# Adaptive-layernorm transformer block, float32, one core: the order of transposes and value matmuls in attention

## The chip, the cores and the metric
One Trainium2 chip, one of its cores. The time is that of the whole program on the device, in microseconds. Three runs of the kernel before gave 970.09, 970.40 and 970.41 us.

## What is computed
x has shape (2, 1024, 256). Cut to what matters:
```python
h = layernorm(x) * (1 + ca) + sa                    # modulation rows from silu(c) @ wmod
q, k, v = split(h @ wqkv.T)                         # 4 groups, 4 query heads each, D = 128
s = where(causal, q @ k.T / sqrt(128), -inf)        # per head 1024 x 1024
x = x + ga * (softmax(s) @ v) @ wproj.T
h = layernorm(x) * (1 + cb) + sb
x = x + gb * ffn(h)                                 # Hadamard transforms, silu gate, 256 -> 1024 -> 256
```
The attention takes from about 45 to 812 us of the span, the feed-forward part the rest.

## The kernel before
Every product is made of float32r pieces: an operand is split into a rounded high part and a low part, and the helper `three` (lines 930 to 935) adds high x high, high x low and low x high. So each tile that leaves TensorE is evicted twice: ACT copies the high part from PSUM, then DVE subtracts it from the same PSUM tile and writes the low part.

**Turns.** Attention runs in 8 turns t, one for each batch and key group. A turn has 8 row blocks i of 128 queries. Row block i has i+1 key blocks j. A unit n is one (row block, key block) pair with its four heads side by side, 512 columns; a turn has 36 units (`UNITS`). They are ordered by four windows of nine units, and window p holds the row blocks 7-p (big) and p (small): row blocks 7 and 0, 6 and 1, 5 and 2, 4 and 3.

**One list for all engines.** `walk` writes one list, `WALK`. TensorE, ACT, DVE and POOL each go through it in order and do their own part of every item, so the order of an engine's instructions follows from the list. The items:
- S (row block, head): TensorE multiplies queries with all keys of the row block (line 1039 and after). DVE adds the mask and takes the maximum (line 831, with a read of its accumulator). ACT does the exp and sums it (line 600). POOL takes the reciprocal and normalises. ACT does not do an exp at its item: `exps()` holds it back until the next S, or until just behind the next T.
- T (unit): TensorE waits until its PSUM bank is free and transposes four 128x128 tiles of probabilities (line 1054). ACT copies pt_hi (line 623), DVE subtracts pt_lo (line 835). There are two banks, used in turn, so a transpose needs the pt_lo of the unit two before it (`ring_free`). pt_hi and pt_lo have three buffers in SBUF.
- V (unit): TensorE waits for pt_lo and multiplies with the value block (lines 933 to 935). Behind the last unit of a row block ACT and DVE split the output (o_hi line 628, o_lo line 840).
- Y (row block): output projection, twelve matmuls of 256 columns, some values after the last V of that row block; DVE adds it to x (line 845).
- C (chunk): one projection of the next turn, six matmuls of 512 columns; VT: transposes of the values (line 1008).
- LF, LN, L, LH, LL: a piece of the second layernorm for two row tiles: statistics and normalisation on DVE, four transposes on TensorE at L (line 957, they use the same two PSUM banks as T), and their evictions.
- W, WM, WP, B: weight splits on POOL.

**The order around the change.** Window p gives each of its units up to two or three items to fill in between: in windows 0 to 2 the scores of the next window, in window 3 the chunks and first scores of the next turn. For a unit the list gets: the first fill item, T, the other fill items, and the V of the unit two before (`LAG` is 2). A V that ends a row block has its Y two values later. In the last turn window 3 has no chunks and no scores to fill in. The score of (i, head) waits in most cases for the exp two scores before, since two PSUM tiles hold scores.

Of the kernel before, what the change touches and what calls it, by code (L numbers as in the profile page):

```python
# [12 lines left out]
B, SEQ, HID = 2, 1024, 256  # L13
# [3 lines left out]
NT = SEQ // P  # L17
# [14 lines left out]
UNITS = []  # L32
for big, small in WINDOWS:
    UNITS += [(big, j) for j in range(HEAD)] + [(small, j) for j in range(small + 1)] + [(big, j) for j in range(HEAD, big + 1)]
NU = len(UNITS)
# [13 lines left out]
LAG = 2  # L49
# [12 lines left out]
CHUNKS_AT = (3, 3, 3, 3)  # L62


def walk():

    def scores(t, i):
        return [(t, "S", i, h) for h in range(QPG)]

    s7 = scores(0, NT - 1)
    out = [(0, "C", 0, 0), (0, "C", 1, 0), (0, "L0", 0, 0), (0, "C", 2, 0), (0, "LH0", 0, 0), (0, "C", 3, 0), (0, "M", 0, 0)]
    out += [(0, "C", c, 0) for c in (4, 5, 6)] + [(0, "G", 0, 0), (0, "C", 7, 0), (0, "WM", 0, 0), (0, "WP", 0, 0)]
    for h in range(QPG):  # L80
        out += [(0, "C", 8 + h, 0), s7[h]]
    for t in range(TURNS):
        s0, s6 = scores(t, 0), scores(t, NT - 2)
        rest = [(t - 1, "Y", i, 0) for i in WINDOWS[-1][::-1]] if t else []
        out += rest[:1] + [(t, "VT", 0, 0)] + s0[3 if t else 0:] + [s6[0]] + rest[1:]
        out += [(t, "WP", 0, 0)] if t else []
        behind, due = [], []

        def value():
            n = behind.pop(0)  # L90
            out.append((t, "V", n, 0))
            if due and due[0][0] == 1:
                out.append((t, "Y", due.pop(0)[1], 0))
            for row in due:
                row[0] -= 1
            if n == LAST[UNITS[n][0]]:
                due.append([3 if n >= NU - 3 else 2, UNITS[n][0]])

        for p, pair in enumerate(WINDOWS):
            units = [n for n, u in enumerate(UNITS) if u[0] in pair]  # L100
            fill = [[] for _ in units]
            if p + 1 < NW:
                for k, item in enumerate([item for i in WINDOWS[p + 1] for item in scores(t, i)][p == 0:]):
                    fill[k + (p == 0 and k > 1)].append(item)
            elif t + 1 < TURNS:
                left = [(t + 1, "C", c, 0) for c in range(NC)]
                for k, many in enumerate(CHUNKS_AT):
                    fill[k] += left[:many]
                    del left[:many]
                for h, item in enumerate(scores(t + 1, NT - 1) + scores(t + 1, 0)[:1]):  # L110
                    fill[len(CHUNKS_AT) + h].append(item)
                fill[1].append((t + 1, "WM", 0, 0))
            if p == 1:
                for k, what in ((0, "LF"), (3, "LN"), (5, "L"), (6, "LH"), (7, "LL")):
                    fill[k].append((t, what, 0, 0))
            if p == 2 and t + 1 < TURNS:
                fill[3].append((t, "W", 0, 0))
            if t + 1 == TURNS and p > 1:
                fill[2].append((t, "B", p - 2, 0))
            for n, extra in zip(units, fill):  # L120
                out += extra[:1] + [(t, "T", n, 0)] + extra[1:]
                behind.append(n)
                if len(behind) > LAG:
                    value()
        while behind:
            if len(behind) == LAG and t + 1 < TURNS:
                value()
                out += scores(t + 1, 0)[1:3]
            value()
        assert [i for _, i in due] == list(WINDOWS[-1][::-1])  # L130
    return out + [(TURNS - 1, "Y", i, 0) for i in WINDOWS[-1][::-1]]


WALK = walk()


# [20 lines left out]
def build(nc, x_in, wqkv, wproj, wmod, c_cols, wug, wdn, su_ug, su_dp, ws_ug, ws_dp, ident_in, mask_in, had_in, out):  # L157
    ctx = ExitStack()
    with ctx:
# [3 lines left out]
        def sem(name):  # L163
            return ctx.enter_context(nc.semaphore(name))
# [80 lines left out]
        T = [psum[2][:, 0:CH], psum[2][:, CH:2 * CH]]  # L245
# [29 lines left out]
        pv_done, oh_done, ol_done = sem("pv_done"), sem("o_hi_done"), sem("o_lo_done")  # L275
# [19 lines left out]
        def this(s, t, k):  # L295

            return (t + 1) * per[s.name] + k
# [11 lines left out]
        def ring(t, what, n=0):  # L309

            return T[TURNED.index((t, what, n)) % 2]
# [31 lines left out]
        def out_slot(i):  # L343

            return FINISHED.index(i) % 2
# [18 lines left out]
        W = [X if n == 1 else T for n in range(len(PIECES))]  # L364
# [56 lines left out]
        def _(pool):  # L421
# [13 lines left out]
            def ln_low(r, b, g, slot):  # L435

                n, block, _, _ = ln_step(r, b, g, slot)
                pool.wait_ge(ln[r]["hi"], n + LN_SLOTS[r] + 1)
                at = bass.ds(block * P, LP * P)
                g_.tensor_tensor(h_lo[:, :, at], h32[slot][:, :, :], h_hi[:, :, at].bitcast(F32), ALU.subtract).then_inc(ln[r]["lo"], 1)  # L440
# [103 lines left out]
        def _(act):  # L544
# [15 lines left out]
            def ln_modulate(r, b, g, slot):  # L560

                n, block, batch, which = ln_step(r, b, g, slot)
                shift, gain = SA + 3 * which, CA + 3 * which
                act.wait_ge(ln[r]["lo"], n + 1)
                act.wait_ge(ln[r]["tr"], n + LN_SLOTS[r] + 1)
                for k in range(KH):
                    last = a_.activation(h32[slot][:, k, :], ln_bank(r, b, g, slot)[:, k * LP * P:(k + 1) * LP * P], ACT.Identity,
                                         scale=cols[:, bass.ds(gain, 1), k, bass.ds(batch, 1)].rearrange("p a b -> p (a b)"),
                                         bias=cols[:, bass.ds(shift, 1), k, bass.ds(batch, 1)].rearrange("p a b -> p (a b)"))
                last.then_inc(ln[r]["h32"], 1)  # L570
# [4 lines left out]
            def v_high(t):  # L575
                for n in range(2):
                    act.wait_ge(vtr_done, this(vtr_done, t, n + 1))
                    a_.activation(v_hi[:, 4 * n:4 * n + 4, :].rearrange("p j d -> p (j d)"), ring(t, "VT", n), ACT.Copy).then_inc(v_hi_s, 1)

            def chunk(t, c):  # L580
                what, h, half = chunks(t)[c]
                act.wait_ge(qkv_done, this(qkv_done, t, c + 1))
                span = slice(half * CH, (half + 1) * CH)
                if what == "v":
                    a_.activation(vt[:, span], bank(t, c), ACT.Copy).then_inc(vt_done, 1)
                elif what == "k":
                    a_.activation(k_hi[:, span], bank(t, c), ACT.Copy).then_inc(qkv_hi, 1)
                else:
                    a_.activation(q_hi[:, h, span], bank(t, c), ACT.Copy, scale=SCALE).then_inc(qkv_hi, 1)  # L589
# [3 lines left out]
            def exps():  # L593

                while waiting:
                    t, i, h = waiting.pop(0)
                    nb, w = halves(i)

                    act.wait_ge(max_done, this(max_done, t, scored(i, h)))
                    a_.activation(row(i, h).rearrange("p (a n) -> p a n", a=nb),  # L600
                                  score_banks(i, h).rearrange("p (a n) -> p a n", a=nb)[:, :, 0:w],
                                  ACT.Exp, bias=nmax[:, place(i), h:h + 1], scale=-1.0,
                                  accum_out=rsum[:, place(i), h:h + 1]).then_inc(exp_done, 1)

            for t, what, n, h in WALK:
                if what == "C":
                    chunk(t, n)
                    exps()
                if what == "L0":
                    for slot in range(2):  # L610
                        ln_modulate(0, 0, 1, slot)
                if what == "VT":
                    exps()
                    v_high(t)
                if what == "L":
                    exps()
                    ln_modulate(1, t // NKV, t % NKV, 0)
                if what == "S":
                    exps()
                    waiting.append((t, n, h))  # L620
                if what == "T":
                    act.wait_ge(t_done, this(t_done, t, n + 1))
                    a_.activation(pt_hi[:, n % 3, :], ring(t, "T", n), ACT.Copy).then_inc(pth_done, 1)  # L623
                    exps()
                if what == "V" and n == LAST[UNITS[n][0]]:
                    i = UNITS[n][0]
                    act.wait_ge(pv_done, this(pv_done, t, n + 1))
                    a_.activation(o_hi[:, out_slot(i), :], O[i], ACT.Copy).then_inc(oh_done, 1)
# [579 lines left out]
```

## Time and profile before
| | us |
|---|---|
| median of three runs | 970.4 |
| the profiled execution, its own time | 970.33 |
| its span, first to last instruction | 968.5 |
| TensorE busy | 941.0 |
| DVE busy | 644.5 |
| ACT busy | 513.8 |
| POOL busy | 456.3 |

Busy time counts each instruction from its recorded start to its recorded end. Matmuls overlap in the records and their ends are modelled, so where a matmul's true length matters, the distance between starts is read. A line of the timeline gives start, length, engine, line of the kernel, operation, out<-in, shape, and how many instructions in a row it stands for; a bracket holds the idle time before it and what ended that.

### The profile page before, as it was taken

To read this page: it belongs to the slowest core of one execution; us is meant where nothing else is said; L and a number is where in the kernel's file an instruction comes from. 1 tells how busy PE (TensorE), PEld (TensorE's weight loads), DVE (VectorE), ACT (ScalarE), POOL (GpSimd) and SP (SyncE) were. 2 spreads that over 40 slices of the span, in tenths; PEclk is the share of its full clock that TensorE was granted. 3 is DMA by queue.
4 is the path that set the end of the run, shared out by engine and by line. 5 is a ranking of instruction groups with operands and counts; after the bars stand their busy time and mean duration, and the time that the engine had idled before them with its cause. 6 is when DMAs were issued, how large, how long until landed. Compare 5 with 4: busy or idle time off the path is not lost.

```text
span 968.5 us, 14525 instructions
## 1 busy us (share of the span) xinstructions
PE 941.0 (97%) x5344; PEld 817.9 (84%) x5344; DVE 644.5 (67%) x1302; ACT 513.8 (53%) x1069; POOL 456.3 (47%) x597
## 2 busy tenths in 40 slices
PE   5889999999999999999999999999999999999997
PEld 5779888988898889888988898889888987888885
DVE  6667757774777477757775777578747876864453
ACT  3266547654765476547654766476646665331121
POOL 1365707670767076707670767076707674120000
PEclk9899999999999999999999999999999999999999
DMA  8000000000001000100000001000000011000000
GB/s 307 23 1 1 33 1 23 2 33 1 23 1 34 1 23 1 33 1 23 1 34 1 23 1 33 1 23 2 1 1 1 1 48 51 1 20 3 22 22 22
DMA packets 9522, 21.14 MB, mean 22 GB/s; under 512 B 1264, under 2 KB 5488, under 8 KB 9328
## 3 DMA queue, kind: packets, MB, share of 16 engines
q1 hardware_dynamic: 8736, 20.19, 6.2%
q8 instruction: 40, 0.66, 0.3%
q14 instruction: 26, 0.21, 0.1%
q10 hardware_dynamic: 720, 0.08, 0.1%
HBM read 18.17 MB, written 2.10 MB: 21 GB/s over the span
## 4 chain that ended last, share of the span: by engine, by line
PE 89%; DVE 7%; ACT 3%; issue 1%; DMA 0%; POOL 0%; DVEq 0%; SPq 0%; ACTq 0%
PE ps L933 19%; PE ps L935 18%; PE ps L934 18%; PE ps L1054 11%; PE ps L1039 7%; PE ps L1045 6%; PE ps L1042 6%; DVE ps L831 3%; ACT prob L600 2%; DVE pt_lo L835 1%; PE ps L957 1%; PE ps L1008 1%; PE ps L1099 1%; PE ps L1100 0%; DMA x<-in_x 0%
## 5 line engine op out<-in xcount | busy, mean ns | idle before, releaser
L493 POOL TENSOR_TENSOR rinv<-rsum,mone 128x1 f32<-128x1 f32 x256 | 142.8, 558 | 274.7 <-ACT prob L600 274.7
L623 ACT ACTIVATE pt_hi<-ps 128x512 fp32r<-128x512 f32 x288 | 171.7, 596 | 134.5 <-PE ps L1054 133.6
L835 DVE TENSOR_TENSOR pt_lo<-ps,pt_hi 128x512 fp32r<-128x512 f32 x288 | 198.2, 688 | 64.3 <-ACT pt_hi L623 62.7
L600 ACT ACTIVATE prob<-ps,nmax 128x1024 f32<-128x1024 f32 (+7 forms) x256 | 189.6, 741 | 81.5 <-DVE nmax L831 80.7
L831 DVE CUSTOM_DVE_ANT_0 ps<-ps,mask_f 128x1024 f32<-128x1024 f32 (+7 forms) x256 | 193.8, 762 | 52.4 <-PE ps L1045 50.6
L496 POOL TENSOR_SCALAR prob<-prob,rinv 128x1024 f32<-128x1024 f32 (+7 forms) x256 | 191.4, 748 | 53.3 <-POOL rinv L493 53.3
L1054 PE MATMUL ps<-ident,prob 128*128 128x128 f32 x1152 | 171.1, 272 | 0.0
L1054 PEld LDWEIGHTS ps<-ident,prob 128*128 128x128 f32 x1152 | 141.1, 140 | 19.1
L933 PE MATMUL ps<-pt_hi,v_hi 128*128 128x512 f32 x288 | 134.3, 466 | 0.0
L935 PE MATMUL ps<-pt_hi,v_lo 128*128 128x512 f32 x320 | 126.3, 395 | 0.0
L1039 PE MATMUL ps<-k_hi,q_hi 128*128 128x512 f32 (+4 forms) x384 | 114.2, 352 | 9.6 <-ACT prob L600 6.7
L934 PE MATMUL ps<-pt_lo,v_hi 128*128 128x512 f32 x288 | 113.5, 394 | 0.0
L1045 PE MATMUL ps<-k_hi,q_lo 128*128 128x512 f32 (+4 forms) x384 | 111.5, 344 | 0.0
L1042 PE MATMUL ps<-k_lo,q_hi 128*128 128x512 f32 (+4 forms) x384 | 110.9, 343 | 0.0
L1039 PEld LDWEIGHTS ps<-k_hi,q_hi 128*128 128x128 f32 x384 | 70.2, 190 | 26.0 <-ACT prob L600 10.8
L794 DVE SCALAR_TENSOR_TENSOR q_lo<-ps,q_hi 128x512 fp32r<-128x512 f32 x64 | 44.1, 691 | 61.0 <-ACT q_hi L589 61.0
L933 PE MATMUL ps<-h_hi,w_hi 128*128 128x512 f32 x192 | 79.3, 413 | 2.8 <-DVE h_lo L747 2.8
L589 ACT ACTIVATE q_hi<-ps 128x512 fp32r<-128x512 f32 x64 | 38.3, 598 | 75.9 <-PE ps L935 75.9
L1042 PEld LDWEIGHTS ps<-k_lo,q_hi 128*128 128x128 f32 x384 | 71.3, 190 | 7.8
L935 PE MATMUL ps<-h_hi,w_lo 128*128 128x512 f32 x192 | 76.3, 397 | 0.0
L934 PE MATMUL ps<-h_lo,w_hi 128*128 128x512 f32 x192 | 76.2, 397 | 0.0
L1045 PEld LDWEIGHTS ps<-k_hi,q_lo 128*128 128x128 f32 x384 | 70.8, 189 | 5.3
(134 smaller groups left out, 1612.8 us busy)
## 6 DMA issues: line engine op xcount, KB each, us to landing
w_raw<-in_wqkv SPq DMA_DIRECT2D x8, 768.0 KB, 4.2
wp_raw<-in_wproj SPq DMA_DIRECT2D x8, 512.0 KB, 3.5
x<-in_x SPq DMA_DIRECT2D x4, 512.0 KB, 10.3
prob<-in_wug SPq DMA_DIRECT2D x4, 512.0 KB, 4.9
out_y<-prob SPq DMA_DIRECT2D x4, 512.0 KB, 2.9
prob<-in_wmod SPq DMA_DIRECT2D x1, 1024.0 KB, 10.2
raw_down<-in_wdn SPq DMA_DIRECT2D x1, 1024.0 KB, 14.0
prob<-in_wmod SPq DMA_DIRECT2D x1, 512.0 KB, 5.3
```

The costliest lines, as they stand in the source:

```text
L496: g_.tensor_scalar(row(i, h), row(i, h), rinv[:, at, h:h + 1], 1.0, ALU.mult, ALU.mult).then_inc(prob_done, 1)
L600: a_.activation(row(i, h).rearrange("p (a n) -> p a n", a=nb), score_banks(i, h).rearrange("p (a n) -> p a n", a=nb)[:, :, 0:w], ACT.Exp, ...
L623: a_.activation(pt_hi[:, n % 3, :], ring(t, "T", n), ACT.Copy).then_inc(pth_done, 1)
L831: v_.tensor_tensor_reduce(scores, scores, late, -1.0, 3.0e38, ALU.add, ALU.min, nmax[:, place(n), h:h + 1]).then_inc(max_done, 1)
L835: v_.tensor_tensor(pt_lo[:, n % 3, :], ring(t, "T", n), pt_hi[:, n % 3, :].bitcast(F32), ALU.subtract).then_inc(ptl_done, 1)
L933: mm(dst, w_h, r_h, start=start, stop=False)
L934: mm(dst, w_h, r_l, start=False, stop=False)
L935: return mm(dst, w_l, r_h, start=False, stop=stop)
L1039: mm(dst[:, a * CH:a * CH + wide], q_hi[:, h, q_at], k_hi[:, a * w:a * w + wide], start=True, stop=False)
L1042: mm(dst[:, a * CH:a * CH + wide], q_hi[:, h, q_at], k_lo[:, a * w:a * w + wide], start=False, stop=False)
L1045: last = mm(dst[:, a * CH:a * CH + wide], q_lo[:, h, q_at], k_hi[:, a * w:a * w + wide], start=False, stop=True)
L1054: last = tr(ring(t, "T", n)[:, q * P:(q + 1) * P], row(i, q, j * P, (j + 1) * P), ident[:, :])
```

## The change
In a turn, units are now taken in pairs (n, n+1), n even, across window borders too. The list gets for a pair: the first fill item of unit n, T n, T n+1, then (but for the first pair) two V, those of the pair before, then all other fill items of both units, the layernorm's L ahead of the rest. The fill items themselves, and the two V behind the last pair, stay what they were. ACT gets one wait: ahead of pt_hi of an odd unit it waits for the V of the unit three before, whose buffer it overwrites.
```diff
--- before.py
+++ after.py
@@ -84,7 +84,7 @@
         rest = [(t - 1, "Y", i, 0) for i in WINDOWS[-1][::-1]] if t else []
         out += rest[:1] + [(t, "VT", 0, 0)] + s0[3 if t else 0:] + [s6[0]] + rest[1:]
         out += [(t, "WP", 0, 0)] if t else []
-        behind, due = [], []
+        behind, due, fill = [], [], [[] for _ in UNITS]
 
         def value():
             n = behind.pop(0)
@@ -97,31 +97,34 @@
                 due.append([3 if n >= NU - 3 else 2, UNITS[n][0]])
 
         for p, pair in enumerate(WINDOWS):
-            units = [n for n, u in enumerate(UNITS) if u[0] in pair]
-            fill = [[] for _ in units]
+            at = p * (NT + 1)
             if p + 1 < NW:
                 for k, item in enumerate([item for i in WINDOWS[p + 1] for item in scores(t, i)][p == 0:]):
-                    fill[k + (p == 0 and k > 1)].append(item)
+                    fill[at + k + (p == 0 and k > 1)].append(item)
             elif t + 1 < TURNS:
                 left = [(t + 1, "C", c, 0) for c in range(NC)]
                 for k, many in enumerate(CHUNKS_AT):
-                    fill[k] += left[:many]
+                    fill[at + k] += left[:many]
                     del left[:many]
                 for h, item in enumerate(scores(t + 1, NT - 1) + scores(t + 1, 0)[:1]):
-                    fill[len(CHUNKS_AT) + h].append(item)
-                fill[1].append((t + 1, "WM", 0, 0))
+                    fill[at + len(CHUNKS_AT) + h].append(item)
+                fill[at + 1].append((t + 1, "WM", 0, 0))
             if p == 1:
                 for k, what in ((0, "LF"), (3, "LN"), (5, "L"), (6, "LH"), (7, "LL")):
-                    fill[k].append((t, what, 0, 0))
+                    fill[at + k].append((t, what, 0, 0))
             if p == 2 and t + 1 < TURNS:
-                fill[3].append((t, "W", 0, 0))
+                fill[at + 3].append((t, "W", 0, 0))
             if t + 1 == TURNS and p > 1:
-                fill[2].append((t, "B", p - 2, 0))
-            for n, extra in zip(units, fill):
-                out += extra[:1] + [(t, "T", n, 0)] + extra[1:]
-                behind.append(n)
-                if len(behind) > LAG:
-                    value()
+                fill[at + 2].append((t, "B", p - 2, 0))
+        for n in range(0, NU, 2):
+            out += fill[n][:1]
+            late = fill[n][1:] + fill[n + 1]
+            out += [(t, "T", n, 0), (t, "T", n + 1, 0)]
+            behind += [n, n + 1]
+            if n:
+                value()
+                value()
+            out += [item for item in late if item[1] == "L"] + [item for item in late if item[1] != "L"]
         while behind:
             if len(behind) == LAG and t + 1 < TURNS:
                 value()
@@ -619,6 +622,8 @@
                     exps()
                     waiting.append((t, n, h))
                 if what == "T":
+                    if n % 2 and n > 1:
+                        act.wait_ge(pv_done, this(pv_done, t, n - 2))
                     act.wait_ge(t_done, this(t_done, t, n + 1))
                     a_.activation(pt_hi[:, n % 3, :], ring(t, "T", n), ACT.Copy).then_inc(pth_done, 1)
                     exps()
```

## Rows read from the trace of the kernel before
**Rows 1.** The page: busy time by engine; granted clock in 40 slices.
```profile
PE 941.0 (97%) x5344; PEld 817.9 (84%) x5344; DVE 644.5 (67%) x1302; ACT 513.8 (53%) x1069; POOL 456.3 (47%) x597
...
PEclk9899999999999999999999999999999999999999
```

**Rows 2.** Waits of TensorE: us in total, times, longest.
```profile
PE ps L1039 <- ACT prob L600: 6.7, 11, 1.9
```

**Rows 3.** Timeline (start, us, engine, line), ACT and TensorE, second score of block 1.
```profile
262.33 1.01 ACT L600 ACTIVATE prob<-ps,nmax 128x896 f32<-128x896 f32 x1 [0.79 <-DVE nmax L831]
...
262.70 0.40 PE L935 MATMUL ps<-pt_hi,v_lo 128*128 128x512 f32 x1
...
263.70 0.28 PE L1042 MATMUL ps<-k_lo,q_hi 128*128 128x256 f32 x1
263.82 0.28 PE L1045 MATMUL ps<-k_hi,q_lo 128*128 128x256 f32 x1
```

**Rows 4.** Timeline, TensorE: values behind transposes, and values behind a projection chunk.
```profile
300.98 0.60 PE L1054 MATMUL ps<-ident,prob 128*128 128x128 f32 x4
301.33 0.48 PE L933 MATMUL ps<-pt_hi,v_hi 128*128 128x512 f32 x1
301.65 0.40 PE L934 MATMUL ps<-pt_lo,v_hi 128*128 128x512 f32 x1
...
302.12 0.40 PE L1039 MATMUL ps<-k_hi,q_hi 128*128 128x512 f32 x1
...
320.24 0.39 PE L934 MATMUL ps<-pt_lo,v_hi 128*128 128x512 f32 x1
...
320.69 0.39 PE L933 MATMUL ps<-h_hi,w_hi 128*128 128x512 f32 x1
```

**Rows 5.** Timeline, TensorE, start of a turn: score, transposes, eight transposes, values.
```profile
254.64 0.57 PE L1039 MATMUL ps<-k_hi,q_hi 128*128 128x448 f32 x2
...
255.86 0.60 PE L1054 MATMUL ps<-ident,prob 128*128 128x128 f32 x4
...
257.52 1.03 PE L1054 MATMUL ps<-ident,prob 128*128 128x128 f32 x8
...
258.63 0.39 PE L934 MATMUL ps<-pt_lo,v_hi 128*128 128x512 f32 x1
```

**Rows 6.** Timeline, ACT, the same stretch.
```profile
256.50 0.60 ACT L623 ACTIVATE pt_hi<-ps 128x512 fp32r<-128x512 f32 x1 [0.73 <-PE ps L1054]
257.25 1.01 ACT L600 ACTIVATE prob<-ps,nmax 128x896 f32<-128x896 f32 x1 [0.16 <-DVE nmax L831]
...
258.25 0.59 ACT L623 ACTIVATE pt_hi<-ps 128x512 fp32r<-128x512 f32 x1
258.92 1.01 ACT L600 ACTIVATE prob<-ps,nmax 128x896 f32<-128x896 f32 x1
```

**Rows 7.** Timeline, DVE, the same stretch.
```profile
257.13 0.69 DVE L835 TENSOR_TENSOR pt_lo<-ps,pt_hi 128x512 fp32r<-128x512 f32 x1
257.74 1.09 DVE L831 CUSTOM_DVE_ANT_0 ps<-ps,mask_f 128x896 f32<-128x896 f32 x1
...
258.87 0.69 DVE L835 TENSOR_TENSOR pt_lo<-ps,pt_hi 128x512 fp32r<-128x512 f32 x1
```

**Rows 8.** Timeline, DVE, ACT and weight loads, window 1: layernorm, 768-wide scores.
```profile
273.55 0.74 DVE L716 BATCH_NORM_STATS2 stats<-x 128x6 f32<-128x256 f32 x2
...
274.80 0.96 DVE L831 CUSTOM_DVE_ANT_0 ps<-ps,mask_f 128x768 f32<-128x768 f32 x1
...
281.14 1.07 DVE L732 TENSOR_SCALAR xhat<-x,mv,rstd 128x256 f32<-128x256 f32 x2
...
282.94 0.68 DVE L835 TENSOR_TENSOR pt_lo<-ps,pt_hi 128x512 fp32r<-128x512 f32 x1
...
275.85 0.90 ACT L600 ACTIVATE prob<-ps,nmax 128x768 f32<-128x768 f32 x1 [0.73 <-DVE nmax L831]
...
283.67 0.42 PEld L957 LDWEIGHTS ps<-ident,xhat 128*128 128x128 f32 x4 [0.26 <-DVE pt_lo L835]
```

## The prediction
> **What bounds the kernel now.** The page first: TensorE is busy 97% of the span at the full granted clock, DVE 67%, ACT 53% [rows 1]. So only two things can move the time: the length of what TensorE executes, and the places where it stands still. The list of TensorE's waits is short: eleven waits of scores on an exp, 6.7 us together [rows 2]. Seven of them are one place, once in each turn but the first (in the timeline always the second score of row block 1): there the value group's last matmul starts at 262.70 and takes 0.23, so TensorE could go on at 262.93; the score's second matmul starts at 263.70, its third 0.12 later, so its first began in truth at 263.58: 0.65 us lost [rows 3]. A second loss stands at the layernorm transposes, which wait 0.26 us for a pt_lo [rows 8]. That is 0.9 us a turn, eight turns. Everything else is TensorE back to back, and ACT and DVE are the engines that feed it.
>
> **Terms, read as start to start.** Transposes of a block (T): the run of eight that already exists at 257.52 has the first value matmul behind it begin at 258.63 - 0.23 = 258.40, so 0.44 for four [rows 5]. Value (V): 3 x 0.233 = 0.70 [rows 4]. An 896-wide score (S): from T at 255.86 to T at 257.52 is 1.66, less 0.44: 1.22 [rows 5]; others by their width, 768 at 1.05, 384 at 0.53, and 256 at 3 x 0.12. ACT and DVE for the same width: TensorE's end to their start 0.20 (T ends 256.30, pt_hi starts 256.50); the exp (e) occupies ACT 257.25 to 258.25 = 1.00; pt_hi (h) start to pt_lo (l) start 258.25 to 258.87 = 0.62 [rows 6, 7]; l holds DVE 257.13 to 257.74 = 0.61; max (m) start to exp start 257.74 to 258.92 = 1.18 [rows 6, 7]; 128 columns less take 0.11 from e and 0.14 from m (busy 0.90 and 0.96 at 768 against 1.01 and 1.09 at 896 [rows 6 to 8]); h holds ACT about 0.49 (0.60 busy, of which the next instruction overlaps 0.1, as it does l's 0.69 to 0.61; estimate). pt_lo start to a transpose that waits for it: 282.94 to the weight load at 283.67, and the matmul just behind it: 0.80 [rows 8]. An exp's start to a score that waits for it: 1.25, as at 262.33 ahead of 263.58 [rows 3].
>
> **Part 1, fewer changes between transposes and matmuls: about 0.3 us a turn saved.** For a saving speaks that the value matmul behind transposes shows 0.48 against 0.40 [rows 4]. But from T's start at 300.98 to V's second matmul at 301.65 is 0.67 = 4 x 0.11 + 0.23: the longer record starts early under the last transpose, and the change itself costs nothing. What is left: two steps behind T take 0.47 (301.65 to 302.12), two in a long stretch of matmuls 0.45 (320.24 to 320.69) [rows 4]. If that excess hangs on the group of transposes and goes with half of them, it is at most 0.025 x 18 groups = 0.45 us a turn; the other bound is 0. I take 0.3, nearer to the upper end since the excess is seen in all triples that I followed.
>
> **Part 2, the two old waits.** L now stands behind two values rather than straight behind its T, and the second score of block 1 gets a whole pair between: taken alone both go, -0.9 us a turn. What becomes late in their place is part 3.
>
> **Part 3, the new order on ACT and DVE.** Both walk the same list. It was S T V, S T V: DVE m l m l, ACT h e h e, so no max stood in a chain with two evictions. Now a pair is F T T V V G (F, G the scores before and behind). DVE: mF l1 l2 mG. ACT: h1 eF h2, and eG only at the next F, ahead of h1'. T(n+2) and T(n+3) need l1 and l2 of the pair before, by the two transpose banks. This closes a relay with no way round: h2, l2, mG, eG, h1', eF', h2'. For 896 wide: 0.62 + 0.61 + 1.18 + 1.00 + 0.49 + 1.00 = 4.90 us a pair. TensorE's pair is 2 x 0.44 + 2 x 0.70 + 2 x 1.22 = 4.72. Each 128 columns less take about a third of a us from both, so the relay is slower than TensorE by 0.18 in every window of scores, and what DVE or ACT do besides (o_hi/o_lo, layernorm) stands in series too. The added wait of h2 for the first value group is 0.70 + 0.20 behind T2, which eF mostly covers; behind h2 stand l2, o_hi, eG. Only Y (twelve 256-wide matmuls at 0.12: 1.44 us) and the projection chunks give slack back.
>
> *Turn start*, by the old rows moved: S 254.64 to 255.86 [rows 5], T0 to 256.30, T1 to 256.74, S to 257.96, T2 to 258.41. l1 cannot be earlier than in the old trace, 258.87, because ACT has h0, e, h1 in front of it [rows 6, 7]; T3 needs it + 0.80 = 259.68. TensorE loses **1.27**; the old order had a V, an S and no wait there.
>
> *Pairs 4 and 6.* m follows l1: 259.48, its e 260.68, h3 261.68, l3 262.30. TensorE: T3, V0, V1 to 261.52, S to 262.74, so the next m 262.94, e 264.14, h4 265.14, l4 265.77, T6 at 266.57; its turn on TensorE was 266.10 (score 0.36, T T 0.88, V V 1.40, two scores 0.72): **0.47**. h5 waits for a 256-wide exp (0.46): 266.09, l5 266.72, T7 at 267.52 against 267.01: **0.51**. Then Y gives 1.4 back; T9 is level.
>
> *Window 1 and L.* From the end of the first 768-wide score it is serial: m 0.87, layernorm front 1.25 (273.55 to 274.80 [rows 8]), m to e 1.05, e 0.89, h 0.49, o_hi to o_lo 0.62 and 0.1 behind l, o_lo 0.6 (as l), m to e 1.05, e 0.89, h 0.49, e 0.89, h to l 0.63, l 0.6, x add 0.34 (estimate: half of l and the fixed part), normalise 0.99 (1.07 busy less the overlap [rows 8]), m to e of 384 0.65, e 0.57, h to l 0.63, and 0.80: 14.6 us with the 0.20 at its head. TensorE has between: three more scores of 1.05, two of 0.53, T T three times (2.64), V V three times (4.2) and Y 1.44, that is 12.5, and 0.25 of waits on the way (the fourth of those scores for its exp, T15 for its bank). L loses **1.85**, plus that **0.25**. It waits for pt_lo of the T just ahead of its values, which the old order had long behind it.
>
> *Windows 2, 3.* Y twice covers most; T27, behind the last score of window 2 with no fill of its own, comes **0.5** early for pt_lo of T25; the second score of the next turn follows four chunks and a score and waits for its bank, **0.25**; V34 and V35 for their pt_lo **0.25**. Chunks are covered: 6 x 0.228 = 1.37 of TensorE against 0.5 of ACT and 0.6 of DVE each.
>
> Sum of a turn: 1.27 + 0.98 + 2.10 + 1.00 = 5.35 of new stops, less the old 0.9 and some 0.2 of small ones at the old turn's end (estimate), less 0.3 of part 1: **+4.0 us**. Seven turns: 28. The last has no chunks; T T V V alone gives pt_lo 1.84 where h2's wait makes 2.33, 0.5 three times less Y's cover, 1.1: +4.7. The profiled span 968.5 becomes 1001.2; the run's own time was 970.3, 1.8 above it, and within 0.1 of the median of 970.4. Forecast **1003 us**. No DMA, no byte and no instruction but one wait is added; w_raw and wp_raw are asked for at places that shift by a unit and have tens of us.
>
> **Rivals.**
> *A, slack holds in all but two places.* Handoffs a little shorter, and the 0.18 never adds up; T3 and L stay (their chains have no way round), the rest goes: (1.27 + 1.85 - 1.1 - 0.3) x 8 = 14, or 984. For it: 0.18 is 4% of a pair, near my reading error. Against: pairs 4 and 6 follow from T3's delay.
> *B, faster.* TensorE's execution decides: the waits go (7.2) and the excess of part 1 too (0.45 x 8 = 3.6): 959.6. It decides if l1 and l2 come inside 2.7 us of their T; for it, 97% busy TensorE and ACT at 53%; against, h1 at 258.25 is forced by the rows. If the whole 0.08 of the longer record were real, 144 x 0.08 = 11.5 more off.
> *C, nothing.* The new stops and the saved ones cancel: 970, if the first chain alone is right.
> *D, the clock.* Stopped 1 to 2 us several times a turn, with eight transposes in a row beside it, TensorE could be granted 1.2 instead of 2.4 GHz for a while. The page has one slice with an 8 in its clock row: 10 to 20% of 24.2 us not granted, 2.4 us at least [rows 1]. Two thirds of that once a turn is 8 x 1.5 = 12 us: 1014. Against it: the row is full in all later slices, with a run of eight transposes in every turn [rows 1, 5].
> The Trainium skill (TensorE: Matmul & The Clock Gate, section Part 4: PE-mode transpose) says that a transpose does not count as TensorE activity for the clock, which speaks against bunching them; by it D would be the outcome. This trace does not bear it out: eight in a row at full clock.
>
> **How the numbers follow.** Forecast 0.62 (its own range 993 to 1012), A 0.18, B 0.08, C 0.04, D or a longer relay 0.08. The range leaves out B, C and most of D: 979 to 1014. A measurement of this kernel tells 0.2% (2 us) from no change: slower 0.88, same 0.04, faster 0.08.
>
> **What would show it.** T3: TensorE idle 1.2 to 1.3 us some 5.2 us behind the turn's value transposes, ended by DVE pt_lo. The layernorm transposes wait for pt_lo 1.5 to 2.3 us, eight times. The score's wait for exp of 0.65 gone. pt_hi waits for an exp, not for a value group. Spacing of T and V unchanged at 0.11 and 0.23. Wrong if pt_lo's total in TensorE's waits is under 10 us, or if the matmul behind transposes turns out to have carried a real cost.

## The result and the profile after

| | before | after |
|---|---|---|
| median of all runs, us | 970.4 (4 runs) | 1004.58 (4 runs, 1004.02 to 1004.89) |
| ratio to before | | 1.035, 95% interval 1.0332 to 1.0368 |
| profiled span, us | 968.5 | 1002.8 |

The change makes the kernel 34.2 us slower; 1003 had been forecast, 979 to 1014 the range.

The page after, for [rows 1]: busy time, granted clock, and the chain that ended last (the work followed back from the last instruction, as shares of the span). Behind it the same chain of the kernel before:

```profile
PE 947.6 (94%) x5344; PEld 820.0 (82%) x5344; DVE 641.6 (64%) x1302; ACT 502.1 (50%) x1069; POOL 454.8 (45%) x597
...
PEclk9899999999999999999999999999999999999999
...
PE 67%; DVE 16%; ACT 12%; issue 4%; DMA 0%; POOL 0%; DVEq 0%; SPq 0%; ACTq 0%
```
```profile
PE 89%; DVE 7%; ACT 3%; issue 1%; DMA 0%; POOL 0%; DVEq 0%; SPq 0%; ACTq 0%
```

All engines have the same number of instructions as before, the clock row is the same, and only TensorE shows more busy time. Its 6.6 us more are not work: a matmul's record is longer than its step (0.39 us against 0.23 at 512 columns), so back to back records overlap, and each new stop pulls two of them apart by up to 0.2 us. What changed is the chain: TensorE carried 89% of the span and now 67%, DVE and ACT together 10% and now 28%. TensorE's waits, for [rows 2] (us in total, times, longest):

```profile
PE ps L1059 <- DVE pt_lo L840: 16.9, 34, 1.1
PE ps L962 <- DVE pt_lo L840: 13.3, 8, 1.7
PE ps L949 <- DMA prob<-in_wmod: 7.2, 1, 7.2
PE ps L1044 <- ACT prob L603: 3.3, 2, 1.9
```

The first two lines are new: the transposes of probabilities (L1059, before L1054) and the layernorm's transposes (L962) stand still for a pt_lo. The scores' wait for an exp is down from eleven times to two, both at the start of the first turn (53.9 and 57.2 us).

One whole turn, from its value transposes to those of the next, first of the kernel before, then after (us, then busy us of TensorE, its weight loads, DVE, ACT and POOL, then the granted clock):

```profile
250.76:347.94 97.18, 96.77 (x579) 85.18 (x578) 66.73 (x137) 58.23 (x125) 53.85 (x71) 1.00 0.05 15
```
```profile
258.93:360.27 101.34, 97.50 (x578) 85.36 (x577) 66.39 (x137) 56.69 (x125) 53.62 (x72) 1.00 0.04 14
```

A turn takes 4.2 us more, at a full clock in both. Over the kernel: 0.2 ahead of the first turn, 3.7 in it, 4.24 in each of the next six, 5.0 from the last turn's value transposes to the end, together 34. The table has the stops of TensorE in one turn. T3 stands for the transposes of unit 3, V34 for the value matmuls of unit 34. Each stop is the distance between the ends of neighbouring matmuls less the usual step; that is some 0.2 us more than the idle time in a bracket of the rows, since the record behind a stop begins early.

| place | forecast | after |
|---|---|---|
| T3 | 1.27 | 1.29 |
| T6, T7 | 0.47, 0.51 | 0.46, 0.51 |
| fourth 768-wide score, T15 | 0.25 | 0.16 + 0.07 |
| layernorm transposes | 1.85 | 1.88 |
| T27 | 0.50 | 0.67 |
| second score of the next turn | 0.25 | 0.38 |
| V34, V35 | 0.25 | 0.14 + 0.17 |
| sum of new stops | 5.35 | 5.73 |
| old stops (0.65, 0.25, 0.2) | -1.1 | -1.1 |
| steps between matmuls (part 1) | -0.3 | -0.4 |
| a turn | +3.95 | +4.2 |

T3 as the trace shows it, for [rows 5], [rows 6] and [rows 7]: TensorE, then ACT, then DVE at the start of the same turn.

```profile
266.12 0.60 PE L1059 MATMUL ps<-ident,prob 128*128 128x128 f32 x4
267.79 0.66 PE L1059 MATMUL ps<-ident,prob 128*128 128x128 f32 x4 [1.07 <-DVE pt_lo L840]
...
264.66 0.60 ACT L628 ACTIVATE pt_hi<-ps 128x512 fp32r<-128x512 f32 x1 [0.73 <-PE ps L1059]
265.42 1.01 ACT L603 ACTIVATE prob<-ps,nmax 128x896 f32<-128x896 f32 x1 [0.16 <-DVE nmax L836]
...
266.42 1.07 ACT L628 ACTIVATE pt_hi<-ps 128x512 fp32r<-128x512 f32 x2
...
265.29 0.69 DVE L840 TENSOR_TENSOR pt_lo<-ps,pt_hi 128x512 fp32r<-128x512 f32 x1
267.04 0.69 DVE L840 TENSOR_TENSOR pt_lo<-ps,pt_hi 128x512 fp32r<-128x512 f32 x1 [1.05 <-ACT pt_hi L628]
```

T2 is over at 266.12 + 0.44 = 266.56. T3 needs the bank of unit 1, so it waits for unit 1's pt_lo. The pt_hi of unit 1 could start only at 266.42, behind the exp at 265.42. Its pt_lo starts at 267.04, and 0.80 later, at 267.84, T3's first transpose really begins (its record starts a little early). 267.84 - 266.56 = 1.28.

The layernorm transposes, for [rows 8]: DVE, ACT, TensorE.

```profile
293.56 1.00 DVE L737 TENSOR_SCALAR xhat<-x,mv,rstd 128x256 f32<-128x256 f32 x2
294.48 0.55 DVE L836 CUSTOM_DVE_ANT_0 ps<-ps,mask_f 128x384 f32<-128x384 f32 x1
...
296.32 0.69 DVE L840 TENSOR_TENSOR pt_lo<-ps,pt_hi 128x512 fp32r<-128x512 f32 x1 [0.71 <-ACT pt_hi L628]
...
295.13 0.58 ACT L603 ACTIVATE prob<-ps,nmax 128x384 f32<-128x384 f32 x1 [2.54 <-DVE nmax L836]
...
295.70 0.58 ACT L628 ACTIVATE pt_hi<-ps 128x512 fp32r<-128x512 f32 x1
...
295.03 0.40 PE L940 MATMUL ps<-pt_hi,v_lo 128*128 128x512 f32 x1
297.07 0.66 PE L962 MATMUL ps<-ident,xhat 128*128 128x128 f32 x4 [1.64 <-DVE pt_lo L840]
```

Read it backwards: the transposes wait for the pt_lo at 296.32, that for the pt_hi at 295.70, that for an exp at 295.13, that for the maximum at 294.48, and that stands behind the normalisation. ACT sat idle for 2.54 us before that exp, although the transposes of unit 14 were over 1.8 us before it (the pair's eight start at 292.92, so the first four end at 293.36). Their pt_hi could have run, but the exp stood in front of it in ACT's order. That is the relay, in one place.

### The profile page after: what moved, and what is told of

The parts are those of the page before. It is cut to its first block, busy times and chain, and to the rows that moved or that the text cites. A ratio compares the mean times of both kernels' runs of the same rounds, so it can differ in the third digit from the quotient of the medians.

```text
span 1002.8 us, 14661 instructions
## 1 busy us (share of the span) xinstructions
PE 947.6 (94%) x5344; PEld 820.0 (82%) x5344; DVE 641.6 (64%) x1302; ACT 502.1 (50%) x1069; POOL 454.8 (45%) x597
## 4 chain that ended last, share of the span: by engine, by line
PE 67%; DVE 16%; ACT 12%; issue 4%; DMA 0%; POOL 0%; DVEq 0%; SPq 0%; ACTq 0%
PE ps L938 15%; PE ps L940 15%; PE ps L939 15%; PE ps L1059 7%; ACT prob L603 7%; DVE ps L836 6%; ACT pt_hi L628 5%; DVE pt_lo L840 4%; PE ps L1044 4%; PE ps L1050 4%; PE ps L1047 4%; DVE xhat L737 1%; PE ps L962 1%; DVE stats L721 1%; PE ps L1013 1%
## 5 line engine op out<-in xcount | busy, mean ns | idle before, releaser
L836 DVE CUSTOM_DVE_ANT_0 ps<-ps,mask_f 128x1024 f32<-128x1024 f32 (+7 forms) x256 | 190.9, 771 | 27.8 <-PE ps L1050 27.1
L1059 PE MATMUL ps<-ident,prob 128*128 128x128 f32 x1152 | 155.7, 274 | 16.9 <-DVE pt_lo L840 16.9
L1059 PEld LDWEIGHTS ps<-ident,prob 128*128 128x128 f32 x1152 | 132.0, 140 | 35.5 <-DVE pt_lo L840 25.6
L938 PE MATMUL ps<-pt_hi,v_hi 128*128 128x512 f32 x288 | 126.2, 438 | 0.0
L938 PE MATMUL ps<-h_hi,w_hi 128*128 128x512 f32 x192 | 76.8, 400 | 2.8 <-DVE h_lo L752 2.8
```

Of the source, the lines that this page charges most:

```text
L836: v_.tensor_tensor_reduce(scores, scores, late, -1.0, 3.0e38, ALU.add, ALU.min, nmax[:, place(n), h:h + 1]).then_inc(max_done, 1)
L938: mm(dst, w_h, r_h, start=start, stop=False)
L1059: last = tr(ring(t, "T", n)[:, q * P:(q + 1) * P], row(i, q, j * P, (j + 1) * P), ident[:, :])
```

## The experiments

**Shorten the relay without touching any order** (cut to what matters).
```diff
-                    scores = ...[:, :, 0:w]
-                    late = mask_f[...]...
+                    scores = ...[:, :, 0:P]
+                    late = mask_f[...]...[:, :, 0:P]
```


> The changed kernel, but DVE adds the mask and takes the maximum over the first 128 columns of each half of a score only (the rest of the row is left out of mask and maximum). TensorE, ACT, POOL and the order of the list are untouched. Theory (the new stops are a relay pt_hi, pt_lo, max, exp, pt_hi, exp over ACT and DVE): each 896-wide max gives 0.68 us back to the relay, so T6 stops for nothing instead of 0.46, T7 0.3 instead of 0.51, T3 1.0 instead of 1.28 (there the exp alone is in front), the layernorm transposes 0.2 instead of 1.86, T27 nothing instead of 0.66: some 3.3 us a turn, about 978 us. Rival (TensorE pays for the grouping itself, or the added wait of pt_hi for the value matmul sets the pace): DVE's max is no part of it, 1004 us.

Measured 973.25 us (ratio to before 1.0035, 1.0023 to 1.0047). TensorE's wait for pt_lo at transposes, in us, times, longest, and after it T3 in one turn:

```profile
PE ps L1059 <- DVE pt_lo L840: 6.9, 10, 0.8
```
```profile
356.32 0.66 PE L1059 MATMUL ps<-ident,prob 128*128 128x128 f32 x4 [0.80 <-DVE pt_lo L840]
```

Stops in a turn: T3 1.02, T6 none, T7 0.31, layernorm 0.25, T27 none; the bank wait of 0.38 (the second score of the next turn) stays. DVE is busy for 64% of the span, so by the busy shares its maximum could cost nothing; yet taking 0.68 us from each 896-wide one gave back 31 us of the 34. The expected 978 was 5 us high.

**The control: the same edit in the kernel before.**


> The control for the kernel with the short maximum: the kernel before (old order) with mask and maximum over the first 128 columns of each half of a score only, the rest left out of them. Theory: in the old order no chain holds a maximum in series, so only the two old waits go (0.65 us in seven turns, 0.25 us in eight): about 963.5 us, 7 us less, against the 31 us that the same edit took off the changed kernel. Rival (DVE's load sets the pace in either order): some 30 us less, 940 us.

Measured 960.3 us (0.9906, 0.989 to 0.9922). A turn takes 96.06 instead of 97.1 us, the first one 2.4 us less. So the same edit is worth 10 us in the old order and 31 us in the new; put the other way, with short maxima the new order costs 13 us (973.25 against 960.3) and not 34. 3 us more than expected went: the small stops at the turn's end (0.2 a turn) and the stalls of the first turn, which had not been counted.

**Take away the added wait.**
```diff
-        pt_hi = sb("pt_hi", [P, 3, CH], F32R)
-        pt_lo = sb("pt_lo", [P, 3, CH], F32R)
+        pt_hi = sb("pt_hi", [P, 4, CH], F32R)
+        pt_lo = sb("pt_lo", [P, 4, CH], F32R)
-                    if n % 2 and n > 1:
-                        act.wait_ge(pv_done, this(pv_done, t, n - 2))
```
(and n % 4 where n % 3 stood)


> The changed kernel with four instead of three buffers for pt_hi and pt_lo, so that the one wait that the change added (ACT ahead of pt_hi of an odd unit, for a value matmul) is gone. Theory: that wait is covered by the exp in front of it in the first seven turns; only in the last turn's fourth window, which has no scores, two stops of 0.50 us ahead of odd transposes go: 1003 to 1004 us. Rival (the added wait is what costs): the time falls by most of the 34 us, to 975 or less.

Measured 1003.04 us. T3, T6, T7 and the layernorm stop are within 0.02 us of the changed kernel's; two waits for pt_lo are fewer:

```profile
PE ps L1057 <- DVE pt_lo L838: 16.0, 32, 1.1
PE ps L960 <- DVE pt_lo L838: 13.2, 8, 1.7
```

A turn takes 101.34 us as before; only the stretch from the last turn's value transposes to the end is shorter, by 1.3 us, where two stops of 0.51 and a part of a third are gone. In the trace that is all that the added wait costs, of 34 us. The cost lies in the order of the list.

**Undo one window at a time.** The units under the condition are listed as in the old kernel; the comment gives the condition of the second run.
```diff
         for n in range(0, NU, 2):
+            if n < 8:                       # old_w0;   8 <= n < 18 in old_w1
+                for one in (n, n + 1):
+                    out += fill[one][:1] + [(t, "T", one, 0)] + fill[one][1:]
+                    behind.append(one)
+                    if one > 1:
+                        value()
+                continue
```


> The changed kernel with the first eight units of each turn (window 0) back in the old order, pairs from the ninth on. Theory: the stops at T3 (1.28), T6 (0.46) and T7 (0.51) belong to the pairs of this window and to nothing else; the old wait of the second score of row block 1 (0.65) comes back; the stops further on stay, the layernorm transposes at 1.86. Net 1.5 to 1.6 us a turn, about 992 us. Rival (a general cost of the new wait or of the pairs, spread over the turn): a fourth of the change's 34 us goes, 996 us, and T3's stop is only moved to the first pair.

Measured 990.5 us (1.0221, 1.0198 to 1.0244). In one turn its only two stops over 0.3 us ahead of window 2 (0.65 and 1.89 by the distances):

```profile
365.47 0.39 PE L1051 MATMUL ps<-k_hi,q_hi 128*128 128x256 f32 x1 [0.39 <-ACT prob L610]
...
389.32 0.66 PE L969 MATMUL ps<-ident,xhat 128*128 128x128 f32 x4 [1.67 <-DVE pt_lo L847]
```

T3, T6 and T7 are gone and do not move to the next pairs, the old 0.65 is back, the layernorm's stop is unchanged: a turn is 1.57 us shorter, as expected.

> The changed kernel with the units 8 to 17 (window 1, which holds the layernorm) in the old order, pairs elsewhere. Theory: the stop at the layernorm transposes goes from 1.86 back to about 0.25, the two small ones ahead of it (0.16, 0.07) go, T3, T6, T7 stay: 1.8 us a turn, about 990 us. Rival (the layernorm's work on DVE is late for its own reasons, whatever the order of T and V): the 1.86 stays and the time is 1002 us or more.

Measured 989.22 us (1.0199, 1.0178 to 1.022); a turn 1.7 us shorter. T3, T6, T7 stand as they were:

```profile
363.40 0.66 PE L1066 MATMUL ps<-ident,prob 128*128 128x128 f32 x4 [1.07 <-DVE pt_lo L847]
370.27 0.66 PE L1066 MATMUL ps<-ident,prob 128*128 128x128 f32 x4 [0.24 <-DVE pt_lo L847]
371.21 0.66 PE L1066 MATMUL ps<-ident,prob 128*128 128x128 f32 x4 [0.29 <-DVE pt_lo L847]
```

and the layernorm waits 0.33 instead of 1.88. From the first turn's value transposes to the end the changed kernel takes 34.1 us more than the kernel before; putting window 0 back takes 11.6 us off that stretch, window 1 13.8. (The medians, 14 and 15 us lower, can also hold a difference from ahead of the first turn, see the last section.) The rest, 8.7 us, lies in windows 2 and 3, if windows act apart from each other; no run puts both back.

**Change only ACT's order.** First everywhere (cut):
```diff
-            def exps():
+            def exps(keep=0):
-                while waiting:
+                while len(waiting) > keep:
...
                 if what == "S":
-                    exps()
+                    exps(1)             # leaves the last one for behind the next pt_hi
                     waiting.append((t, n, h))
```


> The changed kernel, but ACT holds the exp of the score behind a pair back until after the next pair's first pt_hi (before: ahead of it). Nothing is left out. Theory: the relay gets shorter by one pt_hi (0.49) and the first pt_lo no longer stands behind an exp. T3 stays at 1.28 (no held-back exp there). T6 stops for nothing, T7 for 0.5, the layernorm transposes for 0.5 instead of 1.86, T27 for 0.15 instead of 0.66: 2.3 us a turn, about 986 us. Rival (TensorE's order costs by itself): 1004 us.

Measured 1003.93 us: a miss by 18, and the very time that the rival had named. The stops tell the two apart. Those inside the turn fell as the relay says (T6 gone, layernorm 0.87, T3 only 0.49), but a new one took their place at the turn's start, here TensorE and ACT:

```profile
367.19 0.67 PE L1044 MATMUL ps<-k_hi,q_hi 128*128 128x448 f32 x2 [1.24 <-ACT prob L603]
...
369.40 0.66 PE L1059 MATMUL ps<-ident,prob 128*128 128x128 f32 x4 [0.27 <-DVE pt_lo L840]
```
```profile
365.55 0.60 ACT L628 ACTIVATE pt_hi<-ps 128x512 fp32r<-128x512 f32 x1 [2.42 <-PE ps L1059]
366.05 1.00 ACT L603 ACTIVATE prob<-ps,nmax 128x896 f32<-128x896 f32 x1
```

ACT idles 2.42 us, the last 1.9 of them with the exp's maximum finished, since the exp is now listed behind a pt_hi whose transposes are not there yet. The score two behind waits 1.50 for that exp (it really begins at 366.05 + 1.25 = 367.30), and 0.5 and 0.23 go at the turn's last pair. The expectation had followed the held-back exp only where it helped. So:

```diff
-                    exps(1)
+                    follower = WALK[at + 1]
+                    exps(follower[1] == "T" and 0 < follower[2] < NU - 2)
```


> As the kernel that held the exp behind a pair back until after the next pair's first pt_hi, but only where a pair follows and not at a turn's first and last pair, where holding it back had made TensorE wait 1.5 and 0.7 us for an exp. Theory: T3 1.28 as in the changed kernel, T6 none, T7 0.47, the layernorm transposes 0.87 and T17 0.16, T27 0.53: 1.3 us a turn less than the changed kernel, about 994 us. Rival (ACT's order does not matter; what is won at one place is lost at the next): 1003 us.

Measured 997.66 us (1.0286, 1.0264 to 1.0308), 7 us less than the changed kernel where 10 were expected. T3 1.28, T6 none, T7 0.47, layernorm 0.83, T17 0.15, T27 0.54 are as said. But the turn's end still lost: V34 0.61 instead of 0.14, and 0.22 at a score behind the chunks. A turn takes 100.63 us instead of 101.34. With TensorE's list untouched, ACT's order alone is worth 7 us.

**Double the changes between transposes and matmuls, in the kernel before** (cut; the value group thereby also moves ahead of the unit's other fill items).
```diff
                     for q in range(QPG):
+                        if q == 2 and n >= LAG:
+                            value(t, n - LAG)      # the three value matmuls, no longer at item V
```


> The kernel before, but each transpose group is cut in two: two transposes, the three value matmuls of the unit two before, the other two transposes. The number of changes from transposes to matmuls doubles (36 more a turn), each wait stays, no work is left out. Theory (a group of transposes makes the three to four matmuls behind it about 0.006 us slower each, some 0.02 us a group, read from both traces; the pairing saved half of it, 3 us in all): 288 x 0.02 = +5.8 us, about 976 us. Rival (no cost of a change at all; the 3 us came from elsewhere): 970 us. Rival (the longer record of the first value matmul, 0.08 us, is real): 288 x 0.08 = +23 us, 993 us.

Measured 991.89 us (1.0231, 1.0215 to 1.0248). By its time this is the last rival (993 us), by the trace it is not. TensorE in window 1:

```profile
378.28 0.39 PE L1072 MATMUL ps<-ident,prob 128*128 128x128 f32 x2
378.42 0.48 PE L933 MATMUL ps<-pt_hi,v_hi 128*128 128x512 f32 x1
378.73 0.40 PE L934 MATMUL ps<-pt_lo,v_hi 128*128 128x512 f32 x1
...
381.40 0.38 PE L1072 MATMUL ps<-ident,prob 128*128 128x128 f32 x2
382.67 0.62 PE L1055 MATMUL ps<-k_hi,q_hi 128*128 128x384 f32 x2 [0.88 <-ACT prob L600]
```

From the first of two transposes to the second value matmul is 0.45 = 2 x 0.11 + 0.23: the 0.48 record costs nothing here either. All but 1 us of the 21.6 is in stops (in all 54.9 us by the distances, 34.3 before). Nineteen waits of scores for an exp are among them, 13.6 us by the matmul rows, where the kernel before has eleven and 6.7: three value matmuls stand inside a group, so its pt_hi starts 0.7 us later, and the exp stands behind it on ACT.

The disputed term is what matmuls take above their usual step (227 ns at 512 wide) with no stop in it. Summed over all steps within 50 ns of the usual one it is 6.6 us in the kernel before, with 280 groups of transposes in attention, 3.7 us in the changed one with 144, and 7.2 us here with some 530. Halving the groups saved 2.9; nearly doubling them added 0.6 only, so it is not a price per group.

**The kernel before, with its own two waits covered.**
```diff
-                    fill[k + (p == 0 and k > 1)].append(item)
+                    fill[k + (p == 0) * ((k > 1) + (k > 3))].append(item)
...
-                for k, what in ((0, "LF"), (3, "LN"), (5, "L"), (6, "LH"), (7, "LL")):
+                for k, what in ((0, "LF"), (3, "LN"), (6, "LH"), (7, "LL")):
...
+                if p == 1 and n == units[6]:
+                    out.append((t, "L", 0, 0))
```


> The kernel before, in its old order of single units, with its own two waits covered: in window 0 the last three scores of row block 1 come one unit later, and the layernorm transposes stand one unit later, behind a value group and ahead of a score. Nothing is left out. By the two traces these waits cost 0.65 us in seven turns (0.57 or so in the first, which may stay) and 0.25 us in eight: 970.3 - 6.6 = about 963.7 us. If the layernorm transposes only hand their wait on to the next unit's transposes (same two banks), 965.5 us.

Measured 965.78 us (0.9957, 0.9941 to 0.9974). Both waits are gone; a turn takes 96.55 instead of 97.1. One stop of 0.31 is new, ahead of the transposes of unit 6: the pt_lo that they wait for stands behind the same late exp as the score's did, and this is the 2 us by which 963.7 was missed. The layernorm's transposes handed nothing on. So, on top of that edit:

```diff
-                    fill[k + (p == 0) * ((k > 1) + (k > 3))].append(item)
+                    fill[k + (p == 0) * ((k > 1) + (k > 3) - (k == 5))].append(item)
...
-                out += extra[:1] + [(t, "T", n, 0)] + extra[1:]
+                ahead = 2 if n == 6 else 1
+                out += extra[:ahead] + [(t, "T", n, 0)] + extra[ahead:]
```


> The kernel that moved the three scores and the layernorm transposes by a unit, once more changed: it still stopped 0.31 us a turn ahead of the transposes of unit 6, for a pt_lo. Now two scores of row block 1 stand ahead of these transposes rather than one, 0.36 us of TensorE's work in front of the wait. Nothing is left out. Theory: 0.3 us a turn goes, 965.8 - 2.4 = about 963.5 us. Rival (the wait is handed on to the next transposes): 965.8 us.

Measured **963.49 us (0.9939, 0.9926 to 0.9953)**: 0.6% faster than the kernel before, a small difference but clear of its interval, and 4% faster than the changed one. A turn takes 96.27 us. No wait for an engine that comes back every turn is left in the list. The scores' three waits for an exp all lie in the first turn:

```profile
PE ps L1042 <- ACT prob L603: 3.7, 3, 1.9
PE ps L1042 <- DVE q_lo L797: 2.9, 1, 2.9
```

## Why the prediction was right, and where it was not

1. **Part 3, the relay**, was the right mechanism. It rested on the order in which ACT and DVE walk the list, and each stop came within 0.2 us of its working. Four experiments show it: a shorter maximum gives 31 us back and only 10 in the old order; a window put back returns its own stops and leaves the others; ACT's order alone moves 7 us; the added wait is worth 1.3.
2. **Turn start, pairs 4 and 6, layernorm:** 1.27, 0.98, 1.85 forecast; 1.29, 0.97, 1.88 measured. The distance given for recognising T3 in the last section (5.2 us behind the value transposes) contradicts the working, which has it 8.9 us behind; it is 8.9.
3. **The 0.18 us a pair** (4.90 against 4.72) entered no term of the sum, and no run isolates it: a pair with an 896-wide score both ahead and behind stands only at the start of a turn, and the next pair has no score of its own ahead. What made the stops were the first chain of the turn, which had too little time, and what stood in series beside the relay, the layernorm above all.
4. **Windows 2 and 3** were estimated more than followed and came out low: T27 0.67 for 0.50, the bank 0.38 for 0.25, V34 and V35 0.31 for 0.25. With small differences elsewhere the stops of a turn were 0.4 us longer than forecast. Against this stood 0.4 for 0.3 in part 1, and a first turn that lost 3.7 for 4.0; the span was forecast 32.7 us longer and is 34.3 longer. That the miss stayed at 1.6 us is partly these errors of opposite sign.
5. **Part 1:** the size was right (2.9 us in the steps, 2.4 taken, bounds 0 and 3.6). The reason given with it, an excess that hangs on each group, is not: it did not double with the groups. What sets it stays open, so the size was in part luck.
6. **The change between transposes and matmuls itself costs nothing:** right. A transpose steps 0.109 us and the matmul behind it 0.23 in the traces before, after and of the cut groups.
7. **Part 2:** both old waits went, as said. The score's wait stood in the first turn too (0.37 us idle at 69.21), so in all eight and not in seven.
8. **Rival A** (slack in all but two places) failed at T6, T7 and T27; **B** at the first pt_hi of the turn that stands behind an exp, as said. **D**, the clock: it is 1.00 from 75 to 960 us of the changed kernel, with eight transposes in a row in every pair and stops of up to 1.9 us, and ahead of 75 us the two traces have the same lower values (0.86 and 0.93 of two stretches). (Its 1014 should read 1015 by its own sum.) The Trainium skill (TensorE: Matmul & The Clock Gate, Part 4: PE-mode transpose) has it that the full clock does not engage for transposes. This trace does not bear that out for transposes that stand between matmuls.

## What to carry to other kernels

When one list sets the order on several engines, a change of it is to be followed on the engines that are not the bottleneck: write out each one's sequence for a period and add up the loop that closes over the buffers (here 4.90 us by the rows, against TensorE's 4.72), then what stands in series with it, and look first at the places where an engine has just caught up: the start of a turn and the layernorm cost 1.3 and 1.9 us of the 5.7. Averages hid it. ACT at 53% and DVE at 67% had room, and still made TensorE wait, since each takes the list in order and idles in front of an instruction that is not ready (2.54 us at the layernorm) while the next one is. And a matmul record that is longer behind transposes is a matter of where the record begins; the distance between starts decides.

## What was not expected of the hardware

Several of these kernels gave times on two values some 3 us apart. Of 32 runs of the kernel before, taken beside the experiments, seven gave 967.27 to 967.95 and the others 969.87 to 971.01; the kernel of the first edit in the last experiment gave 963.11 once and else 965.68 to 966.40. The shorter runs have a mean granted clock of 0.995 to 0.996, the others 0.992 to 0.995.

One trace shows where such a difference can arise. From 75 to 960 us the clock is 1.00 in the kernel before, the changed one and the two others below. Ahead of that it differs from execution to execution (us; the granted clock of two stretches; start of the first turn's value transposes):

| trace | time | 25 to 50 us | 50 to 75 us | value transposes |
|---|---|---|---|---|
| kernel before | 970.33 | 0.86 | 0.93 | 50.90 |
| changed kernel | 1004.61 | 0.86 | 0.93 | 51.11 |
| waits covered, first edit | 966.40 | 0.86 | 0.86 | 50.87 |
| window 0 put back | 989.22 | 1.00 | 0.86 | 47.30 |

TensorE's instructions up to there are the same in all of them. The last one is one of two short runs of its kernel (989.22 and 988.71, the others 991.78 and 992.07). It had the full clock up to 50 us and is 3.8 us ahead of the changed kernel before attention's first turn begins. So a difference of 2 to 3 us between two medians can come from there (windows put back: 11.6 and 13.8 us by the trace from the first turn on, 14 and 15 by the medians), and small effects are read from the length of a turn. What decides the clock of that stretch in one execution stays open.
